# Twelve units of the up product recomputed on TensorE in the stretch of products, with three load buffers and 40 finished units

## The reference

```python
def act_qdq(x):
    qmax = 2.0 ** (ACT_BITS - 1) - 1.0
    scale = jnp.maximum(jnp.max(jnp.abs(x)) / qmax, 1e-12)
    return jnp.clip(jnp.round(x / scale), -qmax - 1.0, qmax) * scale
...
x = act_qdq(x)
up = act_qdq(x @ lpbq_dequant(w_up).T)
gate = act_qdq(x @ lpbq_dequant(w_gate).T)
sig = fixed_qdq_u16(jax.nn.sigmoid(gate))
gate = act_qdq(gate * sig)
o = act_qdq(gate * up)
return o @ lpbq_dequant(w_down).T
...
x = x + _L0_xattn_ref(_layernorm(x, axis=-1), ctx_1024, itok_BxS_0_511, ...)
x = x + _L0_ffn_ref(_layernorm(x, axis=-1), L0_ffn_w_gate, L0_ffn_w_up, L0_ffn_w_down)
```

## Time and profile before

| | us |
|---|---|
| median of 3 runs | 2354.74 (2351.96 to 2355.8) |
| profiled execution | 2351.6 |
| its span, first to last instruction | 2349.8 |
| opening, gate pass and what leads to them | 0 to about 1149 |
| up pass | 1149 to 1646.4 |
| stretch of products | 1653.2 to 1829.9 |
| down pass, first to last matmul | 1839.5 to 2340 |

### The profile page before, as it was taken

One profiled execution on the slowest core, in us unless ns is written; L12 is line 12 of the kernel. 1 busy time (PEld: TensorE's weight loads), 2 busy tenths in 40 slices (PEclk: granted clock), 3 DMA queues, 4 the chain that ended last, 5 costly groups with the idle time before them and its releaser, 6 DMA issues.

```text
span 2349.8 us, 25399 instructions
## 1 busy us (share of the span) xinstructions
PE 2016.7 (86%) x9524; PEld 944.3 (40%) x9524; DVE 1708.1 (73%) x1368; ACT 1401.7 (60%) x1614; POOL 672.5 (29%) x666
## 2 busy tenths in 40 slices
PE   5888888888499999999999999999000699999998
PEld 2444444444244444444444444444000344444443
DVE  8899999999434534532499998999899744577641
ACT  4688888886422322322499996676899633366530
POOL 2699999998400000000021110222111000000000
PEclk9999999999799999999999999999555799999999
DMA  7789999997346656743699995787998755555541
GB/s 297 309 306 345 340 344 342 340 345 285 120 183 224 229 214 216 255 159 144 240 370 387 382 373 204 263 321 293 400 419 328 292 228 208 205 201 233 233 152 72
DMA packets 131162, 634.60 MB, mean 270 GB/s; under 512 B 12256, under 2 KB 12768, under 8 KB 91104
## 3 DMA queue, kind: packets, MB, share of 16 engines
q1 hardware_dynamic: 85888, 316.81, 37.0%
q0 software_dynamic: 45152, 316.16, 34.7%
HBM read 430.69 MB, written 202.24 MB: 269 GB/s over the span
## 4 chain that ended last, share of the span: by engine, by line
PE 64%; DVE 3%; issue 3%; ACT 2%; DMA 0%; POOL 0%; DVEq 0%; ACTq 0%; POOLq 0%
PE ff_pp L1669 42%; PE ff_pp L1683 21%; ACT ff_ring L1612 1%; DVE ff_sig L1466 1%; DVE ff_h_parts L1450 1%; DVE ff_sq L1388 1%; ACT ff_sig L1599 0%; DMA ff_ab<-hT_scratch 0%; DVE ff_sq L1457 0%; DVE kept_gate L1459 0%; DVE ff_gin L1401 0%; DVE ff_hq L1440 0%; ACT ff_ring L1638 0%; ACT ff_sig L1628 0%; ACT ff_hq L1523 0%
## 5 line engine op out<-in xcount | busy, mean ns | idle before, releaser
L1683 PE MATMUL ff_pp<-kept_down,kept_gate 128*128 128x512 f16 x1536 | 458.8, 380 | 193.1 <-DVE kept_up L1507 193.1
L1669 PE MATMUL ff_pp<-ff_h_parts,kept_gate 128*128 128x512 f16 x2304 | 499.4, 380 | 19.8 <-DVE ff_h_parts L1300 19.8
L1669 PE MATMUL ff_pp<-ff_h_parts,kept_up 128*128 128x512 f16 x2304 | 497.4, 379 | 0.0
L1530 ACT ACTIVATE ff_raw<-ff_pp 128x1024 f32<-128x1024 f32 x192 | 194.3, 1017 | 395.5 <-PE ff_pp L1669 395.5
L1669 PEld LDWEIGHTS ff_pp<-ff_h_parts,kept_gate 128*128 128x128 f16 x2304 | 225.8, 98 | 293.3 <-DVE ff_h_parts L1300 20.2
L1669 PEld LDWEIGHTS ff_pp<-ff_h_parts,kept_up 128*128 128x128 f16 x2304 | 225.4, 98 | 271.8
L1305 DVE TENSOR_REDUCE kept_gate_peak<-ff_raw 128x1 f32<-128x2048 f32 x48 | 109.7, 2286 | 292.3 <-ACT ff_raw L1530 292.3
L1683 PEld LDWEIGHTS ff_pp<-kept_down,kept_gate 128*128 128x128 f16 x1536 | 150.6, 98 | 375.9 <-issue 195.8
L1683 PE MATMUL ff_pp<-kept_down,kept_up 128*128 128x512 f16 x768 | 292.1, 380 | 0.0
L1638 ACT ACTIVATE ff_ring<-ff_hq,kept_g 128x2048 int16<-128x2048 f32 x48 | 96.0, 1999 | 190.3 <-DVE ff_hq L1440 188.8
L699 PE MATMUL at_psO<-kept_wo,at_ahi 128*128 128x512 f16 x512 | 153.7, 382 | 36.1 <-ACT at_alo L264 31.5
(11 more groups left out here) (232 smaller groups left out, 3446.8 us busy)
## 6 DMA issues: line engine op xcount, KB each, us to landing
ff_raw<-up_scratch SPq DMA_DIRECT2D x66, 1024.0 KB, 8.5
gate_scratch<-ff_raw POOLq DMA_DIRECT2D x48, 1024.0 KB, 4.4
ff_gin<-gate_scratch SPq DMA_DIRECT2D x48, 1024.0 KB, 8.6
up_scratch<-ff_raw POOLq DMA_DIRECT2D x48, 1024.0 KB, 7.7
ff_gin<-gate_integers SPq DMA_DIRECT2D x73, 512.0 KB, 6.0
gate_integers<-ff_ring POOLq DMA_DIRECT2D x43, 512.0 KB, 6.6
kept_up<-up_scratch SPq DMA_DIRECT2D x21, 1024.0 KB, 8.9
kept_xs<-in_x SPq DMA_DIRECT2D x32, 512.0 KB, 14.2
```

The lines of the kernel that those rows point to most:

```text
L1530: nc.scalar.activation(raw[:, n % UNITS, h * 2 * BLK:(h + 1) * 2 * BLK], pp[(2 * n + h) % 4][:, :, :].rearrange("p a t -> p (a t)"), ACT.C ...
L1669: mm = nc.tensor.matmul(pp[k % 4][:, h, :], wt[w][:, c, f:f + P], a[:, b % 2, :, c, :], start=(q == 0), stop=(q == len(todo) - 1))
L1683: mm = nc.tensor.matmul(pp[k % 8 // 2][:, k % 2, :], a[b % 2][:, f, t * P:(t + 1) * P], wt[w][:, f, :], start=(q == 0 and i == 0), stop=(q ...
```

## The change

The change has these parts.

- READY goes from 36 to 40: four more gate units are finished in the up pass, which starts this at step 28. In the stretch 8 units are late, 18 "act", 9 "dve", 13 "done" (before: 12, 15, 8, 13).
- The up units of blocks 14, 1, 3 and 5 (`REDO`), twelve in all, aren't loaded in the stretch. TensorE computes them again into the PSUM tiles `pp`, two tiles a unit, and ScalarE takes the magnitude from there, in two instructions of 128 x 1024 instead of one of 128 x 2048. They stand at places 3, 6, 8, 12, 14, 16, 26, 28, 31, 38, 39 and 40.
- The h parts of block 14 are still in SBUF after the up pass. For blocks 1, 3 and 5 SyncE loads the integers again (`load_redo`) and VectorE splits them (`split_again`), after the product of the last place of the block before (places 8, 16 and 31), once TensorE is through with the old parts.
- The up weights and the h parts are needed, so four load buffers go; the 33 up units that are still loaded use the three `raw` alone. One of four small buffers of the gated units (`wq`) goes as well, and the h parts are laid out by block first.
- The list of places is slightly different, since blocks must be asked for in order.

```diff
-READY = 36
+READY = 40
...
+    REDO = [NB - 2, 1, 3, 5]
+    redo = [i for i in range(NU) if order[i] // UNITS in REDO]
+    assert [order[i] for i in redo] == [b * UNITS + q for b in REDO for q in range(UNITS)]
+    from_dram = [i for i in range(NU) if order[i] < NU - UNITS and i not in redo]
...
-    g_slot, g_last = assign({**{("wq", j): -1 for j in range(WQ)}, **residents}, loaded)
-    u_slots, u_last = assign({**{("up", j): -1 for j in range(4)}, **{("raw", n % UNITS): place[n] for n in range(NU - UNITS, NU)}},
-                             from_dram)
+    g_slot, g_last = assign({**{("wq", j): -1 for j in range(1, WQ)}, **residents}, loaded)
+    u_slots, u_last = assign({("raw", n % UNITS): place[n] for n in range(NU - UNITS, NU)}, from_dram)
...
+                def load_redo(y):
+                    sp.wait_ge(m["al"], 2 * NB + y - 1)
+                    sp.dma_start(hq[:, 0, :], hq_d[REDO[y]]).then_inc(hq_in[0], 16)
+
+                load_redo(1)
+                y = 2
                 for i in from_dram:
+                    if y < len(REDO) and i > redo[UNITS * (y - 1) - 1] + 2:
+                        load_redo(y)
+                        y += 1
                     load_up(i)
...
+                def split_again(y):
+                    dve.wait_ge(hq_in[0], 16 * (NB // 2 + y))
+                    dve.wait_ge(m["redone"], UNITS * y)
+                    hi, lo = (t[:, 0].rearrange("p n c t -> p (n c t)") for t in (ah, al))
+                    nc.vector.tensor_copy(hi, hq[:, 0, :]).then_inc(m["ah"], 1)
+                    dve.wait_ge(m["ah"], 2 * NB + y)
+                    nc.vector.tensor_tensor(lo, hq[:, 0, :], hi, ALU.subtract).then_inc(m["al"], 1)
...
+                        if i in redo[UNITS - 1:-1:UNITS]:
+                            split_again(redo.index(i) // UNITS + 1)
...
+                        if i in redo:
+                            x = redo.index(i)
+                            act.wait_ge(m["redone"], x + 1)
+                            nc.scalar.activation(ua[:, i % 3, 0:2 * BLK], pp[2 * x % 4][:, :, :].rearrange("p a t -> p (a t)"),
+                                                 ACT.Abs, scale=g[:, 10:11])
...
+                pe.wait_ge(m["out"], 2 * NB * PAIRS)
+                wt = keep["up"]
+                for x, i in enumerate(redo):
+                    if x >= UNITS and x % UNITS == 0:
+                        pe.wait_ge(m["al"], 2 * NB + x // UNITS)
+                    if x >= 2:
+                        pe.wait_ge(m["ua"], redo[x - 2] + 1)
+                    for k in range(UN):
+                        f = (order[i] % UNITS * UN + k) * P
+                        todo = [(w, a, c) for c in range(DC) for w, a in ((0, ah), (0, al), (1, ah))]
+                        for q, (w, a, c) in enumerate(todo):
+                            mm = nc.tensor.matmul(pp[(2 * x + k // 2) % 4][:, k % 2, :], wt[w][:, c, f:f + P], a[:, 0, :, c, :],
+                                                  start=(q == 0), stop=(q == len(todo) - 1))
+                    mm.then_inc(m["redone"], 1)
                 wt = keep["down"]
-                pe.wait_ge(m["out"], 2 * NB * PAIRS)
```

More of the change, by code:

```diff
@@ L831, in feed @@
     ready = [("kept", v) for v in (KEPT - 1, KEPT - 2, KEPT - 3)]
-    here = [("kept", v) for v in range(KEPT - 3)] + [("ring", v) for v in range(KEPT + LOADED, READY)]
+    here = [("kept", v) for v in (*range(KEPT - 6, KEPT - 3), *range(KEPT - 6))] + [("ring", v) for v in range(KEPT + LOADED, READY)]
     there = [("load", v) for v in range(KEPT, KEPT + LOADED)]
@@ L856, in at_home @@
         return home[:i].count(home[i])
-    from_dram = [i for i in range(NU) if order[i] < NU - UNITS]
+    REDO = [NB - 2, 1, 3, 5]
+    redo = [i for i in range(NU) if order[i] // UNITS in REDO]
+    assert [order[i] for i in redo] == [b * UNITS + q for b in REDO for q in range(UNITS)]
+    from_dram = [i for i in range(NU) if order[i] < NU - UNITS and i not in redo]
     place = {order[i]: i for i in range(NU)}
@@ L919, in feed @@
         junk = flat(sig[:, 1, :]).bitcast(BF16).rearrange("p (r d) -> p r d", d=UE)
-        in_up = floats(keep["up_all"][:, :, :, :])
-        in_h, late_gp = (floats(t_h[:, :, :, :, :, :])[:, i, :] for i in range(2))
+        late_gp = floats(t_h[:, :, :, :, :, :])[:, 1, :]
         oh, ol = ([keep[n][:, a].rearrange("p c f -> p (c f)").rearrange("p (f t) -> p f t", t=BLK) for a in range(2)]
@@ L1050, in u_slot @@
         def u_slot(i):
-            kind, j = u_slots[i][0]
-            return raw[:, j, :] if kind == "raw" else in_up[:, j, :] if j < 3 else in_h
+            return raw[:, u_slots[i][0][1], :]
         def late(n):
@@ L1123, in load_up @@
                     u = order[i]
-                    if prior < 0:
-                        sp.wait_ge(m["mm"], 2 * NB * PAIRS)
-                    else:
-                        sp.wait_ge(m["ua"], prior + 1)
-                    if kind == "raw":
-                        sp.wait_ge(stored[j], 16 * 2 * NB)
+                    sp.wait_ge(m["ua"], prior + 1)
+                    sp.wait_ge(stored[j], 16 * 2 * NB)
                     sp.wait_ge(stored[u % UNITS], 16 * (NB + u // UNITS + 1))
@@ L1241, in load_gated @@
                     pool.dma_start(gated(i), gate_q[u]).then_inc(g_in[kind, j], 16)
-                soon = [i for i in loaded[:WQ] if late(order[i])]
+                soon = [i for i in loaded[:WQ - 1] if late(order[i])]
                 hpk_p(pool)
@@ L1606, in _ @@
                         need(act, m["prod"], i - 2)
-                        if i in from_dram:
-                            act.wait_ge(u_in[u_slots[i][0]], 16 * uses(u_slots, from_dram, i))
-                            from_up = u_slot(i)
-                        else:
-                            from_up = raw[:, order[i] % UNITS, :]
-                        nc.scalar.activation(ua[:, i % 3, :], from_up, ACT.Abs, scale=g[:, 10:11]).then_inc(m["ua"], 1)
+                        if i in redo:
[3 more added lines that the diff above has]
+                                                 ACT.Abs, scale=g[:, 10:11])
+                            nc.scalar.activation(ua[:, i % 3, 2 * BLK:4 * BLK], pp[(2 * x + 1) % 4][:, :, :].rearrange("p a t -> p (a t)"),
+                                                 ACT.Abs, scale=g[:, 10:11]).then_inc(m["ua"], 1)
+                        else:
+                            if i in from_dram:
+                                act.wait_ge(u_in[u_slots[i][0]], 16 * uses(u_slots, from_dram, i))
+                                from_up = u_slot(i)
+                            else:
+                                from_up = raw[:, order[i] % UNITS, :]
+                            nc.scalar.activation(ua[:, i % 3, :], from_up, ACT.Abs, scale=g[:, 10:11]).then_inc(m["ua"], 1)
                     k = i + 1
```

4 lines of the change are left out of this document (2 added, 2 removed).

## The result

The changed kernel takes 2376.3 us (median of 4 runs, 2374.29 to 2377.16); the kernel before took 2353.57 beside it (4 runs). The ratio is 1.0094, 95% interval 1.0081 to 1.0106: slower by 22.7 us. The forecast was 2370 us. The profiled execution took 2374.29 us, its span is 2372.5.

A forecast was written before the change was run, and what follows sets the result against it. The prediction took TensorE's passes and, between them, the balanced VectorE and ScalarE stretch as the bound. Stretch: -6.3 + 18.6 + 3.7 - 2.2 = +13.8 (walk +13.7); with +2.7 into the down pass, +16.4: 2370 us, range 2361 to 2379.

The forecast's parts named there:

- TensorE's units: Stretch between up and down pass: twelve recomputed units, in four groups of three by place, keep VectorE waiting, 18.6 us.
- group 2: Recomputed units at places 12, 14, 16, started after the split behind place 8: products late, loss 11.6 us.
- group 4: Recomputed units at places 38, 39, 40, started after the last split: products late, loss 7.0 us.
- the walk: Hand-written schedule of the stretch from t = 0: last product ends at 190.1 us against 176.4 before, +13.7.
- The clock: TensorE restarts at half clock after gaps of 5 us or more, costing a group's first unit 2.5 to 2.8 us.
- The load behind the h block: SyncE's load for place 19 waits behind an h reload held for the second split; VectorE loses 3.7 us.
- Into the down pass, +2.7: Last product to first down matmul: first loads issued later, 12.0 us where it was 9.3.
- The four early units: Four more units finished in the up pass cost 0 there, at most +3; VectorE's stretch work falls 13.8 us.
- Three buffers: Stretch loads issued three uses ahead, not seven; most in time, losses only 3.7 us at place 19, 0.3 at 11.
- Faster (units never late): Rival: every group of recomputed units is ready before VectorE asks, time 2347 to 2354 us; chance 0.09.
- Clock at full: Rival: TensorE's clock stays full through the stretch's gaps, +11.1 us, 2365; chance 0.12.
- Loads sharing evenly: Rival: loads in flight slow each other evenly, three loads after the h block late, +29 us, 2384; chance 0.10.

The follow-up runs named there:

- Experiment 1: The change with only the high x high products in the recomputation, 16 matmuls a unit for 48: 2358.9 us, ratio 1.0025.
- Experiment 2: The change with extra filling matmuls into a free PSUM bank ahead of TensorE's second, third and fourth groups: 2371.08 us, ratio 1.0074.
- experiment 5: The change with the reloads of h blocks 3 and 5 four places later in SyncE's queue: 2372.4 us, ratio 1.0073.
- Experiment 6: The change with the down pass's first loads reordered and the second up conversion behind the first o tile: 2372.21 us, ratio 1.0085.
- Experiment 4: The kernel before with READY = 40 instead of 36 and nothing else: 2352.99 us, ratio 0.9998.
- experiment 3: The kernel before with its up loads of the stretch through the three raw buffers instead of seven: 2357.05 us, ratio 1.0011.
- experiments 8 and 10: The change with block 14 alone recomputed and the down pass's first loads reordered: 2351.54 us; the same with three more load buffers: 2349.06 us.
- experiment 9: The change with block 14 alone recomputed, first down-pass loads in the change's own order: 2352.73 us, ratio 0.9998.

## Why the prediction was right, and where it was off

The time, 2376.3 us, lies 6.3 above the forecast of 2370 and inside its range. The forecast had +16.4 us between the two passes, and 19.4 were measured there: 2.1 of the difference lie in the stretch, 0.9 on the way into the down pass. Of the 22.7 us of the result 4.0 lie in code ahead of the gate pass and are no part of the forecast mechanism.

- **What bounds the kernel.** Right: 19.4 us of the loss lie between the passes, and the passes themselves are as long as before or 1 us shorter.
- **TensorE's units, 18.6 us of which group 2 had 11.6 and group 4 7.0.** Right in place and size. VectorE's waits at places 12, 14 and 16 sum to 10.6 us, at 38 to 40 to 6.5. Counted as in the prediction, from the reduction of the up peak on (1657.41), the split behind place 8 ends at 32.8 and product 16 at 71.3, where the walk had 32.9 and 71.0. Two things are less neat than the sums. ScalarE waited for TensorE at place 40 but not at place 38; there it was late itself, behind a gate load:

```profile
1805.63 2.00 ACT L1614 ACTIVATE ff_sig<-ff_ab,kept_g 128x2048 f32<-128x2048 int16 x1 [1.08 <-DMA ff_ab<-gate_integers]
```

  So the wait at place 40 is 5.0 us, where the prediction named about 7; without the 1.5 lost at place 38 it would have been that much longer, since the end of TensorE's group is set by the split. And the sum of 18.6 behind evictions in the trace equals the predicted 18.6 by chance: 1.5 of it is the wait at place 26, which isn't TensorE's either. Experiment 1 takes two thirds of the matmuls away and gets 14.0 us back.
- **The clock.** Right: groups 2 and 3 took 2.7 and 3.0 us more than at full clock, group 4 2.2 (2.5 to 2.8 predicted). Experiment 2 shows what it costs the stretch for group 2, not for group 4.
- **The load behind the h block, 3.7 us.** This is the term that was mis-sized. The mechanism was right (experiment 5), the size wasn't: VectorE waited 5.9 us at place 19. I let the two loads run as if they had the engines alone, 3.6 us for the h block and 5.7 for the load behind it; they took 5.6 and 7.7. They weren't alone. GpSimd had issued a gate load 1.6 us ahead of them:

```profile
1729.06 0.53 POOL L1246 DMA_DIRECT2D ff_sig<-gate_integers  x1 [4.16 <-DVE kept_o_peak L1479]
```

  And the reading of the earlier trace rows was too quick: its first load landed at 1651.3 and its fourth at 1663.1, which is 3.9 us apart and not the 2.5 that I took. From place 19 on the trace lies 2.3 to 2.8 us behind the walk, to the end (product 19 starts at 83.5, against 81.1; the third unit of group 3 at 109.0, against 106.2; the last product ends at 192.5, against 190.1). This makes up the miss in the stretch, 15.8 measured against 13.7. The prediction calls the h block in question that of block 3; it is that of block 5.
- **Into the down pass, +2.7.** +3.6 measured, for the same reason: the second up load, which took 6.8 us to land, landed 7.2 us after the last product, and I had let it land 6 after (196.2 against 190.2). Experiment 6 shows that reordering is worth 1 us.
- **The four early units, -13.8 of VectorE's work at no cost in the up pass.** Right in the change, where the tail stays at 6.8 us. Experiment 4 shows how little it stands on: with 40 units the pass ended 5.4 us late in a profile in which VectorE waited 10.4 us for h blocks. It also shows that without the recomputation the stretch got back only 6.3 us for VectorE's 11.6.
- **Three buffers.** Counted only through place 19 and with 0.3 us at place 11, where VectorE waited 1.2 (TensorE's lateness at place 12 covers it). Alone they cost 3.9 us (experiment 3); in the change there are twelve loads fewer.
- **The rest.** 4.0 of the 22.7 us lie ahead of the gate pass, in code that the change doesn't touch: TensorE's matmuls for `at_psQ` and `at_psO`, as many as before, were busy 507 us and not 503. The first gate matmul stood between 649.7 and 651.3 in three profiles of the before's code and between 650.6 and 655.0 in nine of the change's. The nine have the same code there, and they differ by 4.4 us among themselves, so scatter alone could give the 4.0; whether it does stays open. The change and experiments 5 and 6 have sums within 0.9 us of each other and medians that differ by up to 4.1; that can't be put down to the stretch either.
- **Rivals.** Faster (units never late) was seen only with one block recomputed, clear of the interval in experiments 8 and 10. Clock at full: it fell as forecast, and where it was kept up the stretch was 3.4 us shorter. Loads sharing evenly: the loads at place 19 landed 2.0 us late each in company, far from the 15 us of that rival.

## What to carry to other kernels

An idle engine is a gain only if its work is done before the next engine asks for it. Mean load (124 of 177 us here) doesn't tell: ask for each group when its input is there and when its output is wanted. Here three units whose inputs were left over from the pass before cost nothing, and the nine that had to wait for a reload and a split cost 20.2 us of the sum (the change against experiment 9). A loop written out by hand from the pitches of the trace found the 19.4 us between the passes to within 3; what it got wrong were the landings of loads in company.

## What the hardware showed that I had not expected

- The eviction from PSUM with Abs (128 x 1024, fp32 to int16) takes 1.11 us, where the copy to fp32 of the same size takes 1.02. The two differ in function, in output type and in that the scale is read from a column in SBUF; no run tells which of these it is.

```profile
L1625 ACT ACTIVATE ff_ring<-ff_pp,kept_g x12: 1092/1106/1114, 1667.3 to 1820.5; 128x1024 int16<-128x1024 f32 x12
```

- The h block and the load behind it were issued 0.4 us apart, when the DMA engines moved 24 GB/s (1728 to 1730.6) and one gate load had just been issued. From 1730 to 1736 the engines moved 256, 281 and 303 GB/s in slices of 2 us, and each of the two loads landed 2.0 us later than my working from the earlier trace rows had it. With more loads in flight 419 GB/s were reached.
- With the clock at full, a gap of 2.3 us ahead of group 4 in experiment 2 was followed by the half clock, gaps of 1.8 and 1.3 us ahead of groups 2 and 3 were not. The three differ also in what TensorE did ahead of the filling (groups of 144, 144 and 48 matmuls, the 48 after an idle time of 14.5 us), so the length of the gap isn't shown as the cause.
